# Cross attention and a routed feed-forward layer on one core: the attention's order from a list planner, PV products in blocks of two key tiles

## The reference

```
q, k, v = layernorm(x) @ Wq + bq, ctx @ Wk + bk, ctx @ Wv + bv      # 16 heads of 32
attn = softmax(where(mask, q k^T / sqrt(32), -max))
x = x + (attn v) @ Wo + bo
h = layernorm(x)
route_prob = softmax(h @ Ws + bs).T                                 # 8 experts
route_vals, routes = top_k(route_prob, 512)
out = gelu(h[routes] @ W1 + b1) @ W2 + b2
x = x + scatter_add(out * route_vals)
```

## Time and profile before

| | us |
|---|---|
| median of three timed runs | 1729.57 (1729.15 to 1729.82) |
| the profiled execution, span from the first to the last instruction | 1729.0 |
| start of the last PV product, with which the attention stage ends but for its last outputs | 936.3 |
| one batch in the middle (groups 12 to 15) | 113.40 |
| TensorE busy over the whole span | 1620.6 (94%) |
| ScalarE busy over the whole span | 983.9 (57%) |

### The profile page before, as it was taken

The page is one execution under the profiler, slowest core; times in us unless marked ns, Lnnn a source line. Parts: engine busy times, 40 slices in busy tenths (PEclk is TensorE's granted clock), DMA queues, the critical chain, the costliest instruction groups (busy, mean ns, idle before and its releaser), DMA issues.

```text
span 1729.0 us, 22299 instructions
## 1 busy us (share of the span) xinstructions
PE 1620.6 (94%) x7847; PEld 1163.4 (67%) x7847; DVE 1110.7 (64%) x1950; ACT 983.9 (57%) x2115; POOL 303.9 (18%) x396
## 2 busy tenths in 40 slices
PE   7889899899898998999987699999999999999997
PEld 5546566566565664655644488788888888888885
DVE  7576876867768678587664566766454545454543
ACT  5798897987988979888875222223232323232321
POOL 5121221311303112113012010102020202020110
PEclk9999899999999999999989899999999999999999
DMA  5452744635436436263351132435243433334340
GB/s 180 122 170 68 214 120 126 176 96 169 138 92 197 141 123 182 65 205 122 111 183 63 43 123 98 120 107 152 98 139 111 114 131 96 136 99 151 97 123 25
DMA packets 131271, 217.27 MB, mean 126 GB/s; under 512 B 17116, under 2 KB 51056, under 8 KB 131160
## 3 DMA queue, kind: packets, MB, share of 16 engines
q1 hardware_dynamic: 114520, 173.23, 32.3%
q0 software_dynamic: 16640, 42.61, 8.9%
HBM read 157.45 MB, written 57.82 MB: 125 GB/s over the span
## 4 chain that ended last, share of the span: by engine, by line
PE 79%; DVE 9%; ACT 6%; issue 3%; DMA 2%; SPq 0%; POOL 0%; DVEq 0%; POOLq 0%
PE ps_gen L751 8%; PE ps_gen L753 8%; PE ps_gen L752 8%; PE ps_gen L1926 7%; PE ps_gen L1928 7%; PE ps_gen L1927 7%; PE ps_att L1773 6%; PE ps_gen L1730 5%; PE ps_gen L1762 5%; PE ps_gen L1712 3%; ACT ps_gen L1143 3%; PE ps_gen L1713 3%; PE ps_gen L1714 3%; ACT p_ring L1155 2%; DVE stat L1243 2%
## 5 line engine op out<-in xcount | busy, mean ns | idle before, releaser
L1339 DVE TENSOR_REDUCE nmax<-ps_gen 128x1 f32<-128x512 f32 x512 | 338.3, 684 | 128.4 <-PE ps_gen L1730 127.7
L1143 ACT ACTIVATE ps_gen<-ps_gen,nmax 128x512 f32<-128x512 f32 x512 | 343.2, 675 | 57.7 <-DVE nmax L1339 57.7
L1155 ACT ACTIVATE p_ring<-ps_gen,keep_scale 128x512 f32<-128x512 f32 x512 | 336.5, 695 | 61.9 <-PE ps_gen L1762 61.9
L1212 ACT ACTIVATE gel<-ps_gen,b_cols 128x512 f32<-128x512 f32 x128 | 88.3, 690 | 448.8 <-PE ps_gen L753 448.7
L1594 DVE TENSOR_TENSOR gel_lo<-gel,gel_hi 128x512 fp32r<-128x512 f32 x126 | 87.2, 692 | 281.6 <-ACT gel_hi L1213 277.3
L1730 PE MATMUL ps_gen<-kst,qst 97*128 97x512 f32 x512 | 208.2, 429 | 16.8 <-ACT ps_gen L1143 11.2
L1762 PE MATMUL ps_gen<-qst,kst 99*128 99x512 f32 x512 | 195.3, 432 | 16.0 <-ACT ps_gen L1143 11.8
L751 PE MATMUL ps_gen<-hT_hi,w_hi 128*128 128x512 f32 x512 | 202.2, 395 | 0.2 <-DVE hT_lo L1587 0.2
L753 PE MATMUL ps_gen<-hT_hi,w_lo 128*128 128x512 f32 x512 | 199.5, 390 | 0.0
L752 PE MATMUL ps_gen<-hT_lo,w_hi 128*128 128x512 f32 x512 | 199.4, 389 | 0.0
L1926 PE MATMUL ps_gen<-w_hi,gel_hi 128*128 128x512 f32 x504 | 198.1, 393 | 0.0
(11 more groups left out here) (218 smaller groups left out, 2687.4 us busy)
## 6 DMA issues: line engine op xcount, KB each, us to landing
w_raw<-in_L_ffn_W SPq DMA_DIRECT2D x128, 512.0 KB, 3.5
kst<-qk_rows SPq DMA_DIRECT2D x93, 256.0 KB, 3.9
qst<-qk_rows SPq DMA_DIRECT2D x93, 256.0 KB, 5.1
x_in<-in_x POOLq DMA_DIRECT2D x60, 256.0 KB, 3.4
out_x<-x_in SPq DMA_DIRECT2D x32, 256.0 KB, 2.6
qk_rows<-kT_hi SPq DMA_DIRECT2D x31, 256.0 KB, 2.0
qk_rows<-kT_lo SPq DMA_DIRECT2D x31, 256.0 KB, 2.0
qk_rows<-qT_hi SPq DMA_DIRECT2D x31, 256.0 KB, 2.0
```

The source lines that it names most:

```text
L1143: e.activation(psum[:, :], psum[:, :], ACT.Exp, bias=nmax[g % 2][:, c], scale=-1.0, accum_out=den[g % 2][:, c]).then_inc(drained_sem("max" ...
L1155: e.activation(p_ring[n % NP_][:, :], ps("score", g, kt, h)[:, :], ACT.Exp, scale=keep_scale[:, b:b + 1]).then_inc(drained_sem("score", g, ...
L1339: e.tensor_reduce(nmax[g % 2][:, h * TB + t:h * TB + t + 1], ps("max", g, h, t)[:, :], AX.X, ALU.min).then_inc(s_min, 1)
```

## The change

The order of the attention stage now comes from a list planner, `Plan`. Each step is entered once for each engine that has a part in it, with a place (from tables like the old ones, with other numbers, plus a lag), a cost on that engine, the parts that it comes after, and the bank that it takes or gives back. `Plan.run` then hands out parts one by one: of the parts that stand first in their line, the one that can start first, and between equals the one with the earlier place. It keeps at most three `max` banks and two `score` banks taken. Engines thus have orders of their own. The first steps, up to the first scores, stay as they were.

Three things of the program change with it. `att` now covers two key tiles: eight products in one block, behind the exponentials of both. The ring `p_ring` has ten tiles where it had six, and an exponential of tile n waits for the block that read tile n - 10. `oT` holds two groups where it held four: the last two groups of a batch reuse the tiles of the first two, so `osplit` of groups 2 and 3 waits for `outa` of the same batch, and that of groups 0 and 1 for `out` of the batch before. The router's softmax (`choice_max`, `choice_exp`, `choice`, `choice_out`) becomes steps of its own.

```diff
-NP_ = 6
+NP_ = 10
+PAIR = 2
+NPAIR = KT // PAIR
+HALF = GB // 2
...
+class Plan:
...
+    def run(self):
...
+        def startable(part):
+            start = 0.0
+            for need in part.after:
+                before = self.parts.get(need)
+                if before is None:
+                    continue
+                if before.ready is None:
+                    return None
+                start = max(start, before.ready)
+            if part.takes:
+                if not bank_free:
+                    return None
+                start = max(start, min(bank_free.values()) + 0.05)
+                kind = part.takes[0]
+                if kind in HELD:
+                    n = taken[kind] - HELD[kind]
+                    if n >= len(returned[kind]):
+                        return None
+                    if n >= 0:
+                        start = max(start, sorted(returned[kind])[n])
...
+            return max(start, free[part.engine])
...
+                    first = min(start for start, _ in able)
+                    start, part = min((p for p in able if p[0] <= first + LOOK), key=lambda p: (p[1].at, p[0]))
...
+            a.order[part.engine].append(part.step)
...
+LOOK = 0
+HELD = {"max": 3, "score": 2}
...
-    K_AT = ((0.01, 0.35), (-0.13, 0.22), (0.05, 0.15), (0.05, 0.10))
-    Q_AT = ((0.40, 0.42), (0.21, 0.30), (0.14, 0.34), (0.17, 0.32))
-    MAX_AT = ((-0.11, 0.59), (-0.07, 0.66), (-0.05, 0.67), (-0.17, 0.60))
+K_AT = ((-0.013, 0.408), (-0.093, 0.246), (0.177, 0.22), (0.32, 0.331))
+Q_AT = ((0.413, 0.413), (0.33, 0.33), (0.104, 0.278), (0.381, 0.413))
+MAX_AT = ((-0.214, 0.435), (-0.035, 0.769), (0.022, 0.964), (0.232, 0.692))
...
+                p.add("act", ("score", g, kt, h), at,
+                      [("pe", "score", g, kt, h), ("pe", "att", *divmod((n - NP_) // (PAIR * HG), NPAIR))], frees=("score", g, kt, h))
+        for pair in range(NPAIR):
+            kt = PAIR * pair + PAIR - 1
+            p.add("pe", ("att", g, pair), g + (kt + 1) / KT + ATT_AT,
+                  [("act", "score", g, kt, HG - 1), ("dve", "v", b, kt), ("dve", "divide", g - 1)])
...
-        oT = [sb(p1, f"oT_{k}", [P, GB, S], F32R) for k in ("hi", "lo")]
+        oT = [sb(p1, f"oT_{k}", [P, HALF, S], F32R) for k in ("hi", "lo")]
...
-                        on.wait_ge(s_av, (n - NP_) // HG + 1)
+                        on.wait_ge(s_av, (n - NP_) // (PAIR * HG) + 1)
...
-                    if b > 0:
-                        on.wait_ge(*full("outa" if c4 < GB // 2 else "out", b - 1, TB - 1))
-                    e.activation(oT[0][:, c4, :], att_n[:, :], ACT.Identity,
+                    if c4 >= HALF:
+                        on.wait_ge(*full("outa", b, TB - 1))
+                    elif b > 0:
+                        on.wait_ge(*full("out", b - 1, TB - 1))
+                    e.activation(oT[0][:, c4 % HALF, :], att_n[:, :], ACT.Identity,
...
-                    g, kt = at
+                    g, pair = at
                     b, c4 = divmod(g, GB)
-                    on.wait_ge(*drained("score", g, kt, HG - 1))
-                    on.wait_ge(*drained("v", b, kt))
-                    if kt == 0:
+                    tiles = range(PAIR * pair, PAIR * pair + PAIR)
+                    on.wait_ge(*drained("score", g, tiles[-1], HG - 1))
+                    on.wait_ge(*drained("v", b, tiles[-1]))
+                    if pair == 0:
                         on.wait_ge(s_nrm, g)
-                    for h in range(HG):
+                    for kt, h in itertools.product(tiles, range(HG)):
```

More of the change, by code:

```diff
@@ L67, in __init__ @@
         self.steps = []
-        self.times = []
-        self.now = -3.0
+        self.order = {}
         self.bank = {}
@@ L87, in add @@
     def add(self, *step):
-        if self.now < 0 or self.now >= NG:
-            self.now += 1e-4
         self.steps.append(step)
-        self.times.append(self.now)
-    def order_of(self, lags):
-        def at(n):
-            inside = 0 <= self.times[n] < NG
-            return self.times[n] + (lags.get(self.steps[n][0], 0) if inside else 0)
-        return [self.steps[n] for n in sorted(range(len(self.steps)), key=at)]
     def flush(self):
@@ L324, in attention_agenda @@
-    END_MAX_AT, END_ROWS_AT = (-0.39, 0.56), 0.68
-    places = []
-    def place(start, span, calls):
-        lo, hi = start + span[0], start + span[1]
-        for k, call in enumerate(calls):
-            places.append((lo + (hi - lo) * (k + 0.5) / len(calls), call))
-    def late(kind, b, t):
-        if kind == "residual":
-            a.residual(b, t)
-        elif kind == "out":
-            a.out(b, t)
-        elif kind in ("outa", "route", "logits", "back"):
-            a.with_bank(kind, b, t)
-        else:
-            a.add(kind, b, t)
@@ L406, in attention_agenda @@
-    a.now = NG + 1.0
-    attend(NG - 1, KT - 1)
-    for t in range(TB):
-        a.osum(B - 1, t)
-    a.osplit(NG - 1)
-    a.flush()
-    for t in range(TB):
-        a.out(B - 1, t)
-        if t > 0:
-            a.add("x1_norm", B - 1, t - 1)
-    a.add("x1_norm", B - 1, TB - 1)
-    for t in range(TB):
-        a.with_bank("route", B - 1, t)
-    for kind in ("logits", "back"):
-        for t in range(TB):
-            a.with_bank(kind, B - 1, t)
+    a.order = {engine: list(a.steps) for engine in ENGINES}
@@ L1663, in tensor_program @@
             on.wait_ge(s_ident, 2)
-            for kind, *at in steps:
+            for kind, *at in agenda.order["pe"]:
                 if kind == "turn":
```

438 lines of the change are left out of this document (287 added, 151 removed).

## The result

The changed kernel takes **1709.34 us** (median, 1708.42 to 1713.09) against 1729.69 beside it on the same chip: a ratio of 0.9882 [0.9868, 0.9896], 20 us less. Forecast were 1662, 67.5 us less: the direction held, and the time lies just inside the range's upper end, but less than a third of the gain came. The profiled execution is the slowest of the four, 1713.09, with a span of 1711.4, 17.6 under that of before.

What follows compares the result with a forecast made beforehand. TensorE and ScalarE were taken to bound alternate groups, then TensorE all. Batches fall 9.3 us, 55.7 over six; the first and last fall 3.5 and 8.3: 67.5 off span 1729.0, plus 0.6 for the median, 1662; range 1620 to 1710.

Steps and rivals of the forecast that it cites:

- The bound: Attention groups: before, TensorE and ScalarE take turns setting the pace; in the new order TensorE has the larger work in each.
- The balance: Attention batches: the larger engine's work per group, added up, falls from 105.89 to 98.44 us, 5.21 of it TensorE's waiting.
- The maxima's way: Transfer of row maxima to the next group's scores: costed at nothing; with the longest landing 1.3 us missing, at most 10.
- The excess of the second group: Time over TensorE's counted work in a batch's second group: 1.88 us, half way between 0.96 and 2.80.
- The expert stage is not touched: Expert stage after attention: the change was said not to touch it, and it was costed at nothing.
- The fused block: PV block of two key tiles on TensorE: 2.12 us against 2.40 for two, 0.28 saved, 2.24 a batch.
- The whole excess: Time over counted work in a whole batch: 5.7 us in the new order, against 7.51 before; batch of 104.1.
- ScalarE behind the ring: Rival: exponentials wait for whole fused blocks to free tiles, ScalarE loses 1 to 2 us per block; up to 1790, chance 0.14.
- Balance by group only: Rival: work balances by group but not inside it, larger work by key tile falls 109.8 to 105.8; about 1705, chance 0.20.
- No change: Rival: new waits, at the lower clock and at group heads for maxima, cancel the gain; 1726 to 1733 us, chance 0.04.
- A clock of 1.00 in four windows: Sign: TensorE's granted clock has mean 1.00 in each of groups 12 to 15, where one had 0.88 before.
- Few waits for sums: Sign: TensorE seldom waits for ScalarE's sums to give a bank back; no size was given.

Runs made afterwards that it cites:

- a1: The changed kernel with the three first loads of expert weights moved on SP behind the last group's stacking: 1701.9 us, ratio 0.9833.
- a4: The changed kernel with scores that leave out the two rows of the maxima and do not wait for their transfer, which stays: 1691.6 us, ratio 0.9780.
- d1: The changed kernel without the maxima's rows in its scores, 63 of 64 fused PV blocks cut in two with one step between the halves: 1700.7 us, ratio 0.9826.
- d2: The changed kernel, maxima kept, with its fused PV blocks cut in two, one step of TensorE's order between the halves: 1715.2 us, ratio 0.9925.
- b4: The changed kernel with twelve exponential tiles and scores without the maxima's rows; the low part of Wo left out: 1691.1 us, ratio 0.9770.
- b3: The changed kernel in its own order with twelve exponential tiles instead of ten; the low part of Wo left out: 1719.1 us, ratio 0.9926.
- b2: The kernel before, in its order by hand, with only the fused blocks, the ring of ten and the shared output tiles: 1783.1 us, ratio 1.0312.
- d3: The changed kernel with scores without the maxima's rows and the first loads of expert weights last: 1686.3 us, ratio 0.9738.
- c3: The changed kernel, planner's maxima landing price raised from 2.60 to 4.20 us, places searched anew, weight loads last, first maxima row sent at once: 1700.8 us, ratio 0.9817.

## Why the prediction was wrong

**The bound: right. The balance: right, but for the second group of a batch.** TensorE was taken to lead in every group, and it is the busier engine in each. The forecast for a group was its work on TensorE plus an excess; this is how the means of the six middle batches, cut at the first exponentials, came out (a1 has the change's program there, a4 leaves the maxima out):

| group in its batch | forecast | the change | a1 | a4 |
|---|---|---|---|---|
| first | 23.22 | 24.55 | 24.09 | 23.06 |
| second | 30.07 | 33.43 | 32.85 | 32.64 |
| third | 27.14 | 27.96 | 27.54 | 26.37 |
| fourth | 23.69 | 23.69 | 23.69 | 23.44 |

With the maxima out of the way, three groups come at or a little under their forecast, and the second stays 2.6 us over it.

**The maxima's way, "costed at nothing": the step that failed by most in the whole time.** The prediction allowed "1.3 us" in one head of a batch, "at most 10 us", and put none of it into the sum; a4 puts it at 18. It weighed one head, the one behind group 13, against its cover, and that one waits only 0.36 us (434.25). The heads of the fourth groups (7, 11, 15, 19, 27) wait 1.26 to 1.32 us each. And it took the landing from the old order, a median of 1.7; now it is 2.2, up to 5.5, and at those five heads 3.4 to 3.8. The traces show what goes with it. Of the 64 landings, those with a DMA share under 0.3 in the 3 us behind their issue took 1.73 us on the mean before and 1.80 now, those with a share above 0.6 took 3.14 and 3.38. The quick kind were 46 before and are 21 now; the slow kind were 13 and are 23. The order had moved the maxima's way under other transfers. The Trainium skill, "DMA: Bandwidth & Descriptors", in its section on the anatomy of one DMA, gives some 2.0 us of fixed cost, about constant; the median agrees, and the longest here is nearly three times that. Not every late head is a landing: at group 25 (3.44 us) GpSimd issued the second row 3.35 us after the first, for no reason that the profile shows, and it landed in 2.13.

**The excess of the second group (group 1 in the prediction's count): mis-sized.** "Half way, 1.88" was put on it; over its count of 28.19 it measured 5.24, and still 4.45 without the maxima (third group: 2.70 and 1.11). That is 2.6 us a batch, some 15 us in six, that late heads do not explain. In group 13 TensorE stands 2.38 of its 33.84 us, and the mean clock of 0.95 means 3.4 us at half speed, which lost 1.7. The remaining 1.6 is busy time beyond the prices of the count; its source is not shown. TensorE's waits for ScalarE's sums, 1.77 us in each second group, lie all in the group's first half, with and without the maxima.

**"The expert stage is not touched": wrong.** Its loads were: the planner put them ahead of the last group's rows, 7 us (a1). SP's order before and after, read at that place, would have shown it before any run.

**The fused block: price right, worth wrong.** 2.12 us was forecast with entry and exit; the second tile measured 0.86 where 0.92 was taken and 1.00 was the other bound, so 0.34 saved rather than 0.28. The Trainium skill's rule on row groups ("TensorE: Matmul & The Clock Gate", Part 3), which would have given 0.20, does not hold here: the trace has the second tile's weights going in under running products of the same 128 rows. But 64 x 0.28 = 18 us were put into the sum, and d1 and d2 find 8. A saving counts in full only where the engine has no standing time to swallow it, and in d1 the cut showed in the third and fourth groups and not in the second, where TensorE had been standing.

**The whole excess** (5.7 forecast, 11.2 measured: 109.6 - 98.44). a4 brings it to 7.1, b4's best batches to 5.6. With the heads in time the forecast's batch is thus reached at best, not on the mean, and the sum of 5.7 then hides an error each way: the second group is above its forecast, the other three are below theirs. One small price of the count was misread, without consequence: eight logits records stand at 0.40 in the earlier trace rows, not at 0.43, but both orders hold four such steps a batch.

**The rivals.** ScalarE behind the ring came, as two stalls of 1.2 and 2.7 us in each batch and not one at each block, and cost nothing that b3 and b4 could find: the rival took ScalarE's loss for the kernel's. In the order by hand the fused blocks do end slower, by 53 us (b2), but by what step is not shown. *Balance by group only* has the nearest time (1705). Part of its reason is there, in the first half of the second group, where it saw ScalarE ahead: the 1.77 us of waits for sums, 11 us in six batches of the 25 that it allowed. The late heads, which cost more, are not in it, so that its time is that near is luck in part. No change: no.

**The signs.** 64 blocks near 1.92 us: 1.85. ScalarE's waits for scores as long as before: 55.7 against 61.9. A clock of 1.00 in four windows: in three, group 13 has 0.95 (0.88 before). Few waits for sums: 15.8 us in 43 places, under the 23.0 of before's two lines but in more places than their 29. A batch above 110 as proof of error: 109.6, near it. TensorE standing before blocks for exponentials: three times, 7.1 us in all, but in the first and the last batch only (before: four times, 4.0). The clock still falling once a batch: in four of the six middle batches, in the second group.

**What stays open.** With both found terms gone (d3, 1686) 24 us are still missing to 1662. By its windows against the forecast: 5.4 in the first batch (108.34 against 102.9), 12.4 in the middle (106.16 against 104.1), 7.0 from group 28 on (886.60 against 879.6). In the middle it is the second group alone, 32.97 us against 30.07, some 17 us in six batches, while the other three are below their forecast. Ten of the 24 can be the fused blocks' overrated worth (18 - 8), an estimate from d1 and d2. In the change's first batch TensorE stands 3.03 us at 78.33 before a fused block for exponentials. No run takes away only that, or only the waits for sums in the second group.

## What to carry to other kernels

When work is balanced more tightly, check the cover of every transfer at each place where it is waited for, with its landing at the new order's load and not at the old one's, and read each DMA queue for what was moved ahead of what. A stall on an engine that does not set the pace may cost nothing, and a saving on the engine that does may be swallowed by its own waits: only a run that changes that one thing in the same order prices it. A planner's order is as good as its prices: in c3, raising one of them took away the waits that it stands for, and not the time. A forecast by group should be answered by group: here, with the heads in time, three groups of four came in at their figures, and the miss of the second hid in the mean.

## What was not expected of the hardware

In a fused block the second tile's weights of 32 columns go in four records at a time, 0.43 us apart, under running products, and that tile costs 0.86 us where a block alone takes 1.00. The DMAs of the maxima's rows, all of one size and from one queue, land after 1.6 to 5.5 us in one execution, and the DMA share behind their issue goes with it: 1.80 us on the mean under 0.3, 3.38 above 0.6. And the two waits of over 3 us at heads (511.73 and 733.13) are followed by products at half speed, 0.43 us apart, while behind the waits of 1.3 us they stay 0.23 apart. The two batches that hold them take 114.7 and 112.5 us, the other four of the middle 106.4 to 108.2: a late head can cost more than its wait.
